# The decay exponents of an mLSTM layer in fp32r: two parts and 128 rows instead of three bf16 parts and 15 rows

## The reference

```
x_n   = layernorm(x)                       q = x_n, k = v = ctx
ig, fg = [q k v] @ W.T + b                 one value per head and token
cs    = cumsum(log_sigmoid(fg))
log_D = cs[s] - cs[t] + ig[t]  (t <= s)    else -inf
D     = exp(log_D - max_t log_D)
C     = (q k.T / sqrt(32)) * D             per head, 128 x 128
h     = C / (max(|sum C|, exp(-max)) + 1e-6) @ v
x    += layernorm(h) * ln_scale
```

## Time and profile before

| | |
|---|---|
| median of 3 executions | 570.47 us (569.71 to 571.82) |
| the profiled execution | 568.18 us, its span 566.5 us |
| PE (TensorE) busy | 547.5 us, 97% of the span |
| PEld (weight loads) | 447.2 us, 79% |
| DVE (VectorE) | 326.7 us, 58% |
| ACT (ScalarE) | 230.2 us, 41% |
| POOL (GpSimd) | 71.2 us, 13% |
| DMA packets | 59296, of which 37278 under 512 B |
| before stage A's loop | 0 to 25.2 us |
| stage A's loop | 25.2 to 118.7 us |

### The profile page before, as it was taken

One profiled execution on the slowest core, in us unless ns is written; L12 is line 12 of the kernel. 1 busy time (PEld: TensorE's weight loads), 2 busy tenths in 40 slices (PEclk: granted clock), 3 DMA queues, 4 the chain that ended last, 5 costly groups with the idle time before them and its releaser, 6 DMA issues.

```text
span 566.5 us, 8464 instructions
## 1 busy us (share of the span) xinstructions
PE 547.5 (97%) x2773; PEld 447.2 (79%) x2773; DVE 326.7 (58%) x799; ACT 230.2 (41%) x436; POOL 71.2 (13%) x105
## 2 busy tenths in 40 slices
PE   7798998999999999899999999999999999999997
PEld 5566576679888888778888878888878889788887
DVE  6677789768877779773353463434552444542333
ACT  2344545647878844362121361122351122441111
POOL 5232324111412323100000000000000000000000
PEclk9998999999999999999999999999999999999999
DMA  7685537334986999200000100000100000000001
GB/s 206 161 199 175 99 105 185 91 118 169 363 303 204 198 318 229 78 1 0 1 0 1 37 2 1 0 1 0 37 1 1 1 1 19 20 1 0 1 0 39
DMA packets 59296, 47.69 MB, mean 84 GB/s; under 512 B 37278, under 2 KB 50590, under 8 KB 58852
## 3 DMA queue, kind: packets, MB, share of 16 engines
q1 hardware_dynamic: 54264, 30.39, 20.1%
q0 software_dynamic: 4848, 16.78, 9.1%
q10 hardware_dynamic: 148, 0.04, 0.0%
HBM read 40.58 MB, written 2.10 MB: 75 GB/s over the span
## 4 chain that ended last, share of the span: by engine, by line
PE 58%; issue 7%; POOL 2%; DVE 1%; POOLq 0%; DVEq 0%
PE ps L914 57%; POOL rstd L445 1%; POOL h L551 1%; PE ps L584 0%; PE ps L878 0%; DVE qr L1527 0%; DVE x L1515 0%; DVE xn L1275 0%; DVE alT L1554 0%; DVE xT L1282 0%; POOL w L540 0%; POOLq L551 0%; POOL w L542 0%; PE ps L869 0%; DVE ot L1607 0%
## 5 line engine op out<-in xcount | busy, mean ns | idle before, releaser
L914 PE MATMUL ps<-hBt,h 128*128 128x512 f32 x512 | 117.5, 390 | 0.0
L914 PE MATMUL ps<-hA,h 128*128 128x512 f32 x512 | 117.3, 390 | 0.0
L1238 ACT ACTIVATE h<-ps,scol 128x512 f32<-128x512 f32 x64 | 44.2, 690 | 175.3 <-PE ps L914 175.2
L914 PEld LDWEIGHTS ps<-hA,h 128*128 128x128 f32 x512 | 95.9, 188 | 20.4 <-DVE hA L1581 0.6
L914 PEld LDWEIGHTS ps<-hBt,h 128*128 128x128 f32 x512 | 95.8, 188 | 20.3 <-DVE hBt L1581 0.6
L914 PE MATMUL ps<-xT,w 128*128 128x512 f32 x256 | 61.7, 396 | 1.0 <-DVE xT L1282 1.0
L914 PEld LDWEIGHTS ps<-xT,w 128*128 128x128 f32 x256 | 46.2, 188 | 15.0 <-issue 6.0
L1599 DVE CAST hBt<-h 128x512 fp32r<-128x512 f32 x32 | 13.7, 427 | 73.7 <-ACT h L1238 73.7
L1599 DVE CAST hA<-h 128x512 fp32r<-128x512 f32 x32 | 13.7, 427 | 70.0 <-ACT h L1238 70.0
L445 POOL TENSOR_TENSOR rstd<-ve,mhalf 128x4 f32<-128x4 f32 x16 | 16.7, 1041 | 262.9 <-DVE ve L1270 262.9
L1221 ACT ACTIVATE silD<-ps,scol 128x512 f32<-128x512 f32 x32 | 22.1, 689 | 45.2 <-PE ps L914 45.2
(11 more groups left out here) (174 smaller groups left out, 877.2 us busy)
## 6 DMA issues: line engine op xcount, KB each, us to landing
looked<-w_all_in SPq DMA_DIRECT2D x16, 704.0 KB, 5.6
h<-w_all_in POOLq DMA_DIRECT2D x16, 512.0 KB, 6.5
V<-ctx_in SPq DMA_DIRECT2D x32, 128.0 KB, 3.4
Qb<-xT SPq DMA_DIRECT2D x64, 64.0 KB, 2.1
w<-w_all_in POOLq DMA_DIRECT2D x3, 1024.0 KB, 7.7
x<-x_in SPq DMA_DIRECT2D x4, 512.0 KB, 4.2
kstA<-ctxT_in SPq DMA_DIRECT2D x4, 512.0 KB, 5.4
kstC<-ctxT_in SPq DMA_DIRECT2D x4, 512.0 KB, 5.8
```

Source lines behind the costliest of these rows:

```text
L914: last = mm(o, a, b, start=(k == 0 and p == 0), stop=(k == n_k - 1 and p == 1))
L1238: fn(h32[:, m % 2, :], ps[:, 2 + m % 4, :], ACT.Gelu, scale=scol[:, L + 1, m:m + 1])\
```

## The change

Both exponent matmuls become fp32r with 128 rows. Z is split in 2 parts, so `gate_c` has two instructions, not four, and a group's rows are moved by 4 DMAs of twice the bytes each. Lr lies in a region that stage B's context tiles use, so SP waits for the last exponent before it loads kstC. The constants of Rr and Lr come from the chip: POOL fills Lr with -1; ACT loads a small selector `sel` by 2 DMAs and copies it, broadcast, into Rr in 4 instructions (3072, 1024, 2048 and 2048 columns). `tri` is loaded once (32 KB, bf16), copied to fp32r by VectorE, and repeated by the matmul's view.

On TensorE a batch's two exponents come first, each as mask then rows, and then its two scores; in a group's first batch both mask matmuls stand ahead of the wait for `z_moved`. V has rows of 256 channels with 64 ones behind them, loaded by one DMA a group, and `pv` reads two runs of 64 columns (the head's, and the ones).

```diff
-            for part in range(3):
-                sp.dma_start(Rr[part:part + 1, u, :, :, :, :], zp[:, part, 0, :]).then_inc(s["z_moved"], 16)
-                sp.dma_start(Lr[3 + part * Q:3 + part * Q + Q, u, :, :, :], zp[:, part, 1, :])\
-                    .then_inc(s["z_moved"], 16)
+            for part in range(ZP):
+                sp.dma_start(row_of(u, part), zp[:, part, 0, :].bitcast(F32)).then_inc(s["z_moved"], 16)
+                sp.dma_start(columns_of(u, part), zp[:, part, 1, :].bitcast(F32)).then_inc(s["z_moved"], 16)
...
-            for u in range(2):
-                sp.dma_start(Rr[3:RA, u, :, :, :, :], ones_rows_in[3:RA]).then_inc(s["consts"], 16)
-                sp.dma_start(Lr[0:3, u, :, :, :], ones_rows_in[0:3, 0]).then_inc(s["consts"], 16)
-            sp.dma_start(tri[:, :, :], tri_in).then_inc(s["consts"], 16)
+            sp.dma_start(tri_b[:, :], tri_in[:, 0, :]).then_inc(s["tri_ld"], 16)
...
-                for q in range(Q):
-                    sp.dma_start(V[:, u, q, 0:NH, 0:DH],
-                                 ctx_in[Q * g + q].rearrange("t (h d) -> t h d", d=DH)).then_inc(v_ld[u], 16)
+                sp.dma_start(V[:, u, :, 0:D], ctx_in[bass.ds(Q * g, Q)].rearrange("b t d -> t b d"))\
+                    .then_inc(v_ld[u], 16)
...
+            sp.wait_ge(s["expo_done"], UN * G)
             for u in range(2):
                 sp.dma_start(kstC[:, u, :, :], ctxT_in[:, :, u * GT:(u + 1) * GT]).then_inc(ctxT_ld[u], 16)
...
-            nc.gpsimd.memset(V[:, :, :, :, :], 1.0).then_inc(s["const_set"], 1)
+            nc.gpsimd.memset(V[:, :, :, D:], 1.0).then_inc(s["const_set"], 1)
...
+            nc.gpsimd.memset(Lr[:, :, :, :, :].bitcast(F32), -1.0).then_inc(s["lr_set"], 1)
...
+            def causal(quad):
+                mm(ps[:, EX + quad, :], idr[:, :], tri_all, start=True, stop=False)
+
             def expo(g, u, k):
                 q, quad = k // 2, k % 2
                 n = UN * g + k
                 if k == 0:
+                    for a in range(2):
+                        pe.wait_ge(s["d_ready"], n + a + 1)
+                        causal(a)
                     pe.wait_ge(s["z_moved"], MOVES * (g + 1))
-                    pe.wait_ge(s["d_ready"], n + 1)
+                elif k > 1:
+                    if quad == 1:
+                        pe.wait_ge(s["d_ready"], n + 1)
+                    causal(quad)
                 mm(ps[:, EX + quad, :], Lr[:, u, quad, q, :], Rr[:, u, :, quad, q, :],
-                   start=True, stop=False)
-                mm(ps[:, EX + quad, :], idb[:, :], tri[:, :, :], start=False, stop=True)\
-                    .then_inc(s["expo_done"], 1)
+                   start=False, stop=True).then_inc(s["expo_done"], 1)
...
                         for k in (2 * q, 2 * q + 1):
                             expo(g, u, k)
+                        for k in (2 * q, 2 * q + 1):
                             qk(g, u, k)
...
-                        last = mm(ps[:, PV + quad, j * PVW:(j + 1) * PVW], Cts[q % 2][:, quad, j, :],
-                                  V_row[:, par, q, h * VW:h * VW + PVW], start=True, stop=True)
+                        last = mm(ps[:, PV + quad, j * PVW:(j + 1) * PVW].rearrange("p (a w) -> p a w", a=2),
+                                  Cts[q % 2][:, quad, j, :], head_and_ones(par, q, h), start=True, stop=True)
...
+            act.wait_ge(s["sel_zero"], 1)
+            for part in range(ZP):
+                r = ZP + part * Q
+                act.dma_start(sel[r:r + Q, :], ident_in[0:Q, 0:Q]).then_inc(s["sel_ld"], 16)
             table_set(EXP_AND_LN)
+            act.wait_ge(s["sel_ld"], 16 * ZP)
+            rows_fill(0, slice(0, Q - 1))
             k_hi(1, kstA[:, :, :], 0)
+            rows_fill(0, slice(Q - 1, Q))
             x_hi(0, 0)
+            rows_fill(1, slice(0, Q // 2))
             gate_copy(0, QK)
             act.wait_ge(s["gate_copied"], 1)
             act.dma_start(gf[:, :], gsb[NH:2 * NH, :].rearrange("h (q t) -> h q t", q=Q)).then_inc(s["gate_moved"], 16)
+            rows_fill(1, slice(Q // 2, Q))
             log_part(0)
...
                 ch.step(v.tensor_copy(zp[:, 0, :, :], Z[:, :, :]))
                 ch.settle()
-                ch.step(v.tensor_tensor(zr[:, :, :], Z[:, :, :], zp[:, 0, :, :], ALU.subtract))
-                ch.settle()
-                ch.step(v.tensor_copy(zp[:, 1, :, :], zr[:, :, :]))
-                ch.settle()
-                v.tensor_tensor(zp[:, 2, :, :], zr[:, :, :], zp[:, 1, :, :], ALU.subtract).then_inc(s["z_ready"], 1)
+                v.tensor_tensor(zp[:, 1, :, :], Z[:, :, :], zp[:, 0, :, :], ALU.subtract).then_inc(s["z_ready"], 1)
```

More of the change, by code:

```diff
@@ L37 @@
 RA = 3 + 3 * Q
-MOVES = 16 * 6
+ZP = 2
+RZ = ZP + ZP * Q
+MOVES = 16 * 2 * ZP
 MASKED = 1e30
@@ L124, in two_layers @@
         kstC = place([stage_at[0]], "kstC", [P, 2, KD, GT], F32)
+        Lr = place([stage_at[0]], "Lr", [P, 2, 2, Q, S], F32R)
         silD = place(stage_at, "silD", [P, 2, GT], F32)
@@ L128, in two_layers @@
         idf = place(base, "idf", [P, P], F32)
-        idb = place(base, "idb", [P, P], BF16)
-        tri = place(base, "tri", [P, Q, S], BF16)
+        idr = place(base, "idr", [P, P], F32R)
+        tri = place(base, "tri", [P, S], F32R)
+        tri_b = place(base, "tri_b", [P, S], BF16)
+        sel = place(base, "sel", [P, Q], F32)
         lns = place(base, "lns", [P, D], F32)
@@ L198, in two_layers @@
         a3 = [r2b[0]]
-        Rr = place(a3, "Rr", [RA, 2, Q, 2, Q, S], BF16)
-        Lr = place(a3, "Lr", [RA, 2, 2, Q, S], BF16)
-        gsb = place(a3, "gsb", [2 * NH, GT], F32)
+        Rr = place(a3, "Rr", [P, 2, Q, 2, Q, S], F32R)
+        g3 = [gate_at[0]]
+        gsb = place(g3, "gsb", [2 * NH, GT], F32)
         NR = NH * Q
[L203 to L214, removed]
+        gi = place(g3, "gi", [NR, S], F32)
+        gf = place(g3, "gf", [NR, S], F32)
+        gb = place(g3, "gb", [NR, 2], F32)
+        fab = place(g3, "fab", [NR, S], F32)
+        fmn = place(g3, "fmn", [NR, S], F32)
+        fl = place(g3, "fl", [NR, S], F32)
+        one_r = place(g3, "one_r", [NR, S], F32)
+        cs = place(g3, "cs", [NR, S], F32)
+        Z = place(g3, "Z", [NR, 2, S], F32)
+        zp = place(g3, "zp", [NR, ZP, 2, S], F32R)
+        Er = place(g3, "Er", [NR, S], F32)
+        assert g3[0] <= spill_at
         b3 = [r2b[0]]
@@ L325, in _ @@
                     .then_inc(s["x_rest"], 16)
-            for part in range(3):
+            sp.wait_ge(s["rows_set0"], 2)
+            for part in range(ZP):
                 part_made(sp, part)
-                sp.dma_start(Rr[part:part + 1, 0, :, :, :, :], zp[:, part, 0, :]).then_inc(s["z_moved"], 16)
+                sp.dma_start(row_of(0, part), zp[:, part, 0, :].bitcast(F32)).then_inc(s["z_moved"], 16)
             queries_in(0, 0, 1)
@@ L372, in _ @@
                     sp.wait_ge(s["av_done"], Q * g + Q)
[L373 to L376, removed]
+                    values(g, u)
                     sp.wait_ge(s["mask_free"], g + 1)
@@ L435, in settle @@
                 pool.wait_ge(s["pool_own"], own[0])
+            nc.gpsimd.memset(sel[:, :], 0.0).then_inc(s["sel_zero"], 1)
             step(nc.gpsimd.memset(mhalf[:, :], -0.5))
@@ L571, in _ @@
             mm = nc.tensor.matmul
+            tri_all = tri[:, :].rearrange("p (j t) -> p j t", j=1).to_broadcast([P, Q, S])
             pe.sem_inc(s["qk_done"], 4)
@@ L1086, in flag_sum, with rows_fill @@
                 fn(facc[:, 0:2 * G], facc[:, 0:2 * G], ACT.Copy, accum_out=fsum[:, 0:1]).then_inc(s["flag_sums"], 1)
+            def rows_fill(u, js):
+                fn(Rr[:, u, js, :, :, :].rearrange("p j a q t -> p j (a q t)"),
+                   sel[:, js].rearrange("p (j o) -> p j o", o=1).to_broadcast([P, js.stop - js.start, 2 * Q * S]),
+                   ACT.Copy).then_inc(s[f"rows_set{u}"], 1)
+            act.wait_ge(s["sel_zero"], 1)
+            for part in range(ZP):
+                r = ZP + part * Q
+                act.dma_start(sel[r:r + Q, :], ident_in[0:Q, 0:Q]).then_inc(s["sel_ld"], 16)
             table_set(EXP_AND_LN)
+            act.wait_ge(s["sel_ld"], 16 * ZP)
+            rows_fill(0, slice(0, Q - 1))
             k_hi(1, kstA[:, :, :], 0)
+            rows_fill(0, slice(Q - 1, Q))
             x_hi(0, 0)
+            rows_fill(1, slice(0, Q // 2))
             gate_copy(0, QK)
@@ L1097, in _ @@
             floor_part(0)
-            for part in range(3):
+            act.wait_ge(s["lr_set"], 1)
+            for part in range(ZP):
                 part_made(act, part)
-                act.dma_start(Lr[3 + part * Q:3 + part * Q + Q, 0, :, :, :], zp[:, part, 1, :])\
-                    .then_inc(s["z_moved"], 16)
+                act.dma_start(columns_of(0, part), zp[:, part, 1, :].bitcast(F32)).then_inc(s["z_moved"], 16)
             with act.Fori(0, 2) as i:
@@ L1400, in _ @@
             dve.wait_ge(s["ident_ld"], 16)
```

(4 more changed lines are left out.)

44 lines of the change are left out of this document (26 added, 18 removed).

## The result

The change gave 3.3 us, not 9.1. In 22 runs of each kernel on the same chips the new one took a median of 568.66 us (565.76 to 572.62), the one before 571.98 (568.88 to 576.40): a ratio of 0.9943, 95% interval [0.9922, 0.9964]. The forecast was 561.4, range 557.5 to 567.5.

The account below looks back on a forecast made before the run. TensorE, busy 97% of the span, was taken as the bound, with VectorE nearly as loaded in stage A. Gains of 1.8 + 2.3 + 2.0 + 1.3 + 1.7 = 9.1 us took the median of 570.47 to 561.4, range 557.5 to 567.5.

Parts of the forecast that it names:

- Part 1: Stage A's exponent matmuls: as fp32r they take 0.23 us each, not 0.32; 1.8 us of 5.8 counted as gain.
- The rival of bare loads: Weight loads of the 64 exponent matmuls not hidden, 0.58 us apiece: 16.6 us more, about 580; chance 0.06.
- the order is worth no more than the pitch: TensorE's masks ahead of rows: second score 0.3 us earlier, first 0.3 later, so nothing counted beyond the shorter matmul spacing.
- Part 2: Z in two parts: `gate_c` loses a subtraction and a cast, 0.76 us in each of groups 0 to 2; 2.3 us.
- Part 3: SP at group boundaries: two fewer row moves bring the next queries 1.2 us earlier; with the third boundary, 2.0 us gained.
- Part 4: Before the loop: earlier gates' rows and shorter `gate_c` land the row moves at 23.9, not 25.2; 1.3 us gained.
- Part 5: Clock in group 1: the first of two 1.2 GHz stretches goes, 1.7 us gained; bounds -1.7 (a third comes) to 3.0.
- the sum of part 5: Clock loss reckoned as window length times missing clock share: group 1's 26.8 us x 0.13 = 3.5 us lost.
- Part 6: V read in two runs and loaded without short packets: 0 us counted, 1.5 gained in stage C as the other end.
- VectorE and the DMAs hold what TensorE gives: Rival in stage A: TensorE comes earlier but waits longer; 5.5 us remain, 563.5 to 567; chance 0.25.
- the start eats it: Rival before the loop: late selector, colliding fills, moves no earlier, clock unchanged; 3 us or less gained, 567 to 570; chance 0.09.

Follow-up runs that it names:

- e17: The changed kernel with TensorE's old order: exponents and scores quad by quad, rows' wait ahead of the first mask; 570.48 us, ratio 0.9994.
- e9: The changed kernel with x's loads for groups 2 and 3 issued ahead of the queries' first batch; 566.23 us, ratio 0.9890.
- e10: The changed kernel with POOL's weight loads at a group's start and x's loads ahead of the first queries; 565.04 us, ratio 0.9874.
- e12: The changed kernel with a group's four weight loads issued singly and x's loads ahead of the first queries; 563.72 us, ratio 0.9838.
- e8: The changed kernel with POOL's four weight loads issued at a group's start, behind `k_lo`; 569.13 us, ratio 0.9950.
- e1: The changed kernel with POOL's four weight loads issued at a group's end, behind the last `h_root`; 574.51 us, ratio 1.0025.
- e14: The changed kernel with early weights and x as in e10, but V loaded by four DMAs a group; 570.42 us, ratio 0.9963.
- e16: The kernel before the change, with the load schedule of e12 (single weight loads, x early); 577.24 us, ratio 1.0119.
- e11: The kernel before the change, with the load schedule of e10 (weights at a group's start, x early); 578.81 us, ratio 1.0104.
- e18: The changed kernel with V loaded by four DMAs a group, not one; 568.61 us, ratio 0.9953.
- e19: The changed kernel with a group's four weight loads issued singly, x's loads left in place; 565.50 us, ratio 0.9907.

## Why the prediction failed

**Part 1, right in mechanism.** TensorE, then its weight loads, after:

```profile
30.00 0.39 PE L635 MATMUL ps<-tri,idr 128*128 128x512 f32 x1
30.23 0.39 PE L649 MATMUL ps<-Rr,Lr 128*128 128x512 f32 x1
30.45 0.39 PE L635 MATMUL ps<-tri,idr 128*128 128x512 f32 x1
```

```profile
30.00 0.19 PEld L649 LDWEIGHTS ps<-Rr,Lr 128*128 128x128 f32 x1
30.23 0.19 PEld L635 LDWEIGHTS ps<-tri,idr 128*128 128x128 f32 x1
```

The matmuls come 0.23 apart and each load lies under the matmul before, against 0.32 with 0.37 idle. The rival of bare loads is out. The sentence that the order is worth no more than the pitch failed: it is worth 2.9 us (0.8 to 5.0), most or all of the 3.3 that the change gave. I had weighed 0.3 later against 0.3 earlier for the scores, and not that masks under a DMA's wait shorten TensorE's idle stretch. That the clock gives the rest is argued: two of the low stretches in e17 stand behind such waits.

**Part 2, right in what `gate_c` saves.** VectorE after: `zp` is made in two operations.

```profile
20.37 0.27 DVE L1356 CAST zp<-Z 32x256 fp32r<-32x256 f32 x1
20.68 0.41 DVE L1358 TENSOR_TENSOR zp<-Z,zp 32x256 fp32r<-32x256 f32 x1
```

**Part 3, the step that failed.** "The queries' first batch has landed at 48.88 [...] VectorE's gain brings both earlier alike": I took the landing as the issue plus a constant, and left the DMAs' own limit to the lower bound of 0, from a mean share of 81% over a whole group. The mean hides the 6 us at the boundary at 1.1 to 1.2. There an issue 2.6 us earlier moved the first score by 0.1 only (48.75, not 48.88), where 45 was forecast. At the third boundary TensorE and VectorE came 2.5 earlier (`turn_x` at 95.22, not 97.77), but after the wait of 2.48 for Qb the first score is only 0.8 earlier (99.67, not 100.51), and the low stretch behind that wait takes this too. So the 2.0 us of part 3 were not there.

**Part 4, wrong by the same step.** The gates landed at 17.27, `log_part` began at 17.89, ACT's fills were hidden, all as forecast or better. The moves were issued at 20.7 to 22.1 (forecast 20.9 to 22.4). They landed at 25.33, not 23.9: x's two loads, issued at 18.49, held the engines at 0.99 of their time from 20 to 22. With x ahead (e9) the loop starts at 24.27, and at 23.82 in e10, so the step's size was right once the engines were free.

```profile
15.72 1.91 ACT L1114 ACTIVATE Rr<-sel 128x2048 fp32r<-128x2048 f32 x1 [0.93 <-ACT gsb L1082]
17.89 0.31 ACT L1087 ACTIVATE fl<-fab 32x128 f32<-32x128 f32 x1 [0.26 <-DVE fab L1334]
18.49 1.20 SPq L332 DMA_DIRECT2D x<-x_in  x2
20.74 1.38 ACTq L1140 DMA_DIRECT2D Lr<-zp  x2
```

**Part 5** hung on part 3: the idle stretch stayed, and the low clock with it. The other one went and a third came in group 3, which the forecast had as its lower bound. By the sum of part 5, 27.0 x 0.06 + 22.2 x 0.08 = 3.4 us are lost after, 3.5 before: an estimate of 0.1 gained for 1.7 counted. With the waits gone (e12) all three are gone. But a long wait alone does not bring the low clock: e8's trace has waits of 2.86 and 2.76 us and a mean clock of 0.999, and the second low stretch of the kernel before had no wait over 0.65 just ahead. What decides it is open.

**Part 6** is not settled. The two runs that were to test the short packets have none. They show that the number of V's loads costs nothing measurable in the change as made, and 5.1 us in e10. What the short packets cost stage A or C is open.

**The base.** 561.4 stood on a median of three, 570.47; 22 runs give 571.98. Of the error of 7.3 us, 1.5 is the base and 5.8 the lost gain. The rival "VectorE and the DMAs hold what TensorE gives" (563.5 to 567) had the mechanism but not the size: it named VectorE's load as its reason, and the DMA engines did it. The rival "the start eats it" (568 to 570) holds the measured 568.66, in part by luck: the moves landed no earlier and the clock lost as much as before, as it says, but the selector was in time, and x's megabyte, not the moves' bytes, kept the rows late. That the reschedule brings 9.3 us, near the 9.1 of the sum, is no proof of the terms one by one: the sum has nothing for the order, which is worth 2.9 by itself. Open: what the pitch alone is worth, which was not tried by itself, what `gate_c` and the start gave in the change as made, and what the short packets cost.

## What to carry to other kernels

A transfer issued earlier lands earlier only if the DMA engines have room at that new time: before counting such a gain, read the share of the DMA engines in windows of 2 us around it, and list what every other queue issues there. Where a load without a hurry meets one with a hurry, issue it in single pieces between other work, ahead of where it is read; moving it as a whole moves the wait. When a run is to put a cost back in, see in its trace that the cost is there: four loads did not bring the short packets back. Take the base from many runs, and give matmuls that can run under a wait a place there.

## What the runs showed of the hardware

- The queries' loads (64 KB, 128 partitions) landed 2.0 us after issue with POOL's weights elsewhere (e1), 2.7 issued behind most of their 1.5 MB (before), 5.3 issued in them (after), 6.5 in e14.
- With runs of 32 channels into V's rows of 33 (1024 packets of 128 B a load), the issue itself stretches: four V loads cost SP 2.93 us in the kernel before, at a mean DMA share of 0.54 meanwhile, 4.94 in e16 at 0.79, and 6.70 in e11 at 1.09. Four loads without such packets cost 1.98 in e14 and in e18, one load 0.42.
- The scatter between executions goes with the clock. In the 22 runs of the changed kernel the time falls by about 5.3 us per 0.01 of mean granted clock (0.987 at 572.1, 0.996 at 565.8 to 567.6; correlation -0.79). That is no fixed price: the 12 runs of e14 give 1.5 us per 0.01 (-0.57), those of e17 7.0 (-0.89).
- From VectorE's last operation to the end the program took 2.1 us in four profiled executions (before, e9, e18, e19) and 3.5 to 4.3 in the others, with the same code.
